# QKV stage: the remainders of queries and keys are formed by VectorE instead of GpSimd

## What is computed

```python
x = x + 0.5 * ffn(layernorm(x))
x = x + attn(layernorm(x))
x = x + 0.5 * ffn(layernorm(x))
```

```python
qkv = clip(einsum('bsd,ed->bse', layernorm(x), Wqkv), -8, 8)
q, k, v = split(qkv, 3)
q = layer_norm(q, q_ln_w, q_ln_b)        # over all 512 features
k = layer_norm(k, k_ln_w, k_ln_b)
scores = q @ k.T * 16 ** -0.5 + bias     # per head, 32 heads of 16
```

## Time and profile before

| | |
|---|---|
| median of 3 runs | 1060.15 us (1060.13 to 1060.8) |
| the profiled execution | 1064.33 us |
| its span, from first to last instruction | 1062.6 us |
| mean granted clock of TensorE, share of full speed | 0.924 |
| busy over the span: TensorE | 876.8 us, 83% |
| VectorE | 652.9 us, 61% |
| ScalarE | 446.5 us, 42% |
| GpSimd | 352.6 us, 33% |
| QKV stage, TensorE's first to last projection matmul | 274 to 459 us |

### The profile page before, as it was taken

The page is one execution under the profiler, slowest core; times in us unless marked ns, Lnnn a source line. Parts: engine busy times, 40 slices in busy tenths (PEclk is TensorE's granted clock), DMA queues, the critical chain, the costliest instruction groups (busy, mean ns, idle before and its releaser), DMA issues. The chain is left out here.

```text
span 1062.6 us, 20207 instructions
## 1 busy us (share of the span) xinstructions
PE 876.8 (83%) x6688; PEld 646.4 (61%) x6689; DVE 652.9 (61%) x1296; ACT 446.5 (42%) x818; POOL 352.6 (33%) x342
## 2 busy tenths in 40 slices
PE   2667699994698888858999999999859974699994
PEld 2556588873576776635555555555447763588873
DVE  6647244431988887757777777777427667344432
ACT  2332233331244343335777777777723430133321
POOL 4550577764022122120000000000024440577764
PEclk9997799997799999967999999999978995799998
DMA  8784578773244479664666666655148872378773
GB/s 247 268 276 119 165 142 153 140 134 50 82 152 150 154 194 207 179 203 103 145 134 140 132 138 133 140 132 112 33 140 264 292 246 99 85 142 154 135 136 52
DMA packets 112859, 162.08 MB, mean 153 GB/s; under 512 B 16864, under 2 KB 74336, under 8 KB 112512
## 3 DMA queue, kind: packets, MB, share of 16 engines
q1 hardware_dynamic: 94928, 123.85, 42.4%
q0 software_dynamic: 17856, 37.25, 19.1%
HBM read 97.44 MB, written 67.37 MB: 155 GB/s over the span
## 5 line engine op out<-in xcount | busy, mean ns | idle before, releaser
L827 DVE TENSOR_REDUCE att_part<-att_s_ps 128x2 f32<-128x1024 f32 (+2 forms) x160 | 195.4, 1225 | 61.4 <-PE att_s_ps L675 60.9
L789 ACT ACTIVATE att_prob<-att_st_ps 128x512 f32<-128x512 f32 x320 | 173.7, 595 | 78.7 <-PE att_st_ps L701 78.7
L143 PE MATMUL exp_z_ps<-ex_w_hi,exp_xT_hi 128*128 x312 | 131.7, 422 | 2.3 <-issue 1.0
L145 PE MATMUL exp_z_ps<-ex_w_hi,exp_xT_lo 128*128 x312 | 125.7, 403 | 0.0
L144 PE MATMUL exp_z_ps<-ex_w_lo,exp_xT_hi 128*128 x312 | 125.3, 402 | 0.0
L1470 DVE TENSOR_TENSOR exp_xT_lo<-exp_t_ps,exp_xT_hi 128x512 fp32r<-128x512 f32 x78 | 53.9, 692 | 106.7 <-ACT exp_xT_hi L1456 106.7
L1463 ACT ACTIVATE exp_y<-exp_y 128x512 f32<-128x512 f32 x72 | 45.5, 632 | 171.8 <-DVE exp_y L1482 171.8
L1099 POOL TENSOR_TENSOR ex_w_lo<-ex_bias,ex_w_hi 128x1024 fp32r<-128x1024 f32 x32 | 77.0, 2409 | 92.6 <-ACT ex_w_hi L1203 92.4
L1398 POOL DMA_INDIRECT exp_xg<-xn,ex_token_of x78 | 78.2, 1002 | 88.1 <-SPq L1370 60.4
L714 PE MATMUL att_pv_ps<-att_prob,att_v_sb 128*32 128x256 f32 (+2 forms) x1280 | 101.4, 391 | 1.8 <-ACT att_oT L794 1.8
L639 POOL CAST att_m_parts<-att_part 128x28 fp32r<-128x28 f32 x32 | 6.6, 208 | 271.3 <-DVE att_part L831 271.3
(11 more groups left out here) (199 smaller groups left out, 1713.4 us busy)
## 6 DMA issues: line engine op xcount, KB each, us to landing
ex_bias<-in_L_ffn_W_e SPq DMA_DIRECT2D x32, 512.0 KB, 6.8
v_vals<-st_vals SPq DMA_DIRECT2D x16, 512.0 KB, 2.8
q_parts<-st_partq SPq DMA_DIRECT2D x32, 256.0 KB, 3.4
k_parts<-st_partk SPq DMA_DIRECT2D x32, 256.0 KB, 3.8
att_v_sb<-v_vals SPq DMA_DIRECT2D x32, 256.0 KB, 3.7
ex_bias<-in_L_attn_hidden_states SPq DMA_DIRECT2D x8, 512.0 KB, 5.0
acc<-ex_bias SPq DMA_DIRECT2D x8, 512.0 KB, 7.3
xn<-route_xn SPq DMA_DIRECT2D x8, 512.0 KB, 5.9
```

The costliest lines, as they stand in the source:

```text
L143: nc.tensor.matmul(out, x_hi[:, s], w_hi(c), start=(c == 0), stop=False)
L145: last = nc.tensor.matmul(out, x_lo[:, s], w_hi(c), start=False, stop=(c == C - 1))
L789: nc.scalar.activation(prob[n % 2][:, col:col + 512], st_ps[(e + half) % 3][:, :], ACT.Exp).then_inc(exp_done, 1)
L827: nc.vector.tensor_reduce(out, src, X_AXIS, ALU.max, negate=True).then_inc(red_done, 1)
```

## The change

GpSimd's loop over the tiles is removed; GpSimd keeps its constants at the start of the stage. VectorE has a new function `rest` that forms one remainder, with the same waits and the same semaphore. In step t it runs `rest(t - 1, ..., 0)` between the normalised keys and the clip of values, and `rest(t - 1, ..., 1)` behind the clip of values; the two of the last tile stand behind the loop. VectorE's first four tiles are written out instead of two.

```diff
-            def step(t, par):
-                for s in range(2):
-                    pool.wait_ge(part_hi, 2 * t + s + 1)
-                    at_least(pool, qk_stored[par], STORES * (t // 2))
-                    nc.gpsimd.tensor_tensor(parts[s][1][par][:, :, :], whole[s][par][:, :, :], parts[s][0][par][:, :, :].bitcast(F32),
-                                            ALU.subtract).then_inc(part_lo, 1)
-            tile_loop(pool, step)
...
+            def rest(t, par, s):
+                dve.wait_ge(part_hi, 2 * t + s + 1)
+                at_least(dve, qk_stored[par], STORES * (t // 2))
+                nc.vector.tensor_tensor(parts[s][1][par][:, :, :], whole[s][par][:, :, :], parts[s][0][par][:, :, :].bitcast(F32),
+                                        ALU.subtract).then_inc(part_lo, 1)
...
             def step(t, par):
                 unit(t, par)
+                if after(t, 1):
+                    rest(t - 1, 1 - par, 0)
                 clip(t, par, 2)
-            tile_loop(dve, step)
+                if after(t, 1):
+                    rest(t - 1, 1 - par, 1)
+            tile_loop(dve, step, first=4)
+            for s in range(2):
+                rest(TILES - 1, 1, s)
```

## The result

The changed kernel takes 1047.27 us (median of 4 runs, 1046.89 to 1049.02) against 1060.47 (1060.13 to 1063.36, 4 runs) for the kernel before on the same chip: 13.2 us less. The recorded ratio is 0.9866, 95% interval 0.9842 to 0.9891; the quotient of the two medians, 0.9876, lies inside it. The profiled execution went from 1064.33 to 1049.02 us, its span from 1062.6 to 1047.3.

A forecast was written before the change was run, and what follows sets the result against it. VectorE, held partly by GpSimd, bounds the QKV stage. Gains of 6.8 us until tile 8's clip of values, 2.5 in steps 9 to 13, then 0.6 and 1.3 sum to 11.2: 1060.15 - 11.2 = 1049.0 us; range 1046.0 to 1054.6.

The forecast's parts named there:

- more is gained: Rival: VectorE's idling shrinks and TensorE keeps 2.4 GHz in the tail, giving 1046.5 to 1047.5 us; 17%.
- Blocking: GpSimd's subtractions hold VectorE's small instructions (L80, L85) until they end; removing them saves 2.0 us per ordinary step.
- The remainder's price: Each 128x512 subtraction moved to VectorE costs 0.60 us start to start, 1.2 us per step.
- The ordinary step: QKV loop step: 11.45 - 2.0 + 1.2 = 10.65 us, VectorE still bounding since TensorE needs 9.94.
- Steps 1 to 4: Early QKV steps: gains of 0.85 us in step 1, 2.4 in steps 2 and 3, 0.35 in step 4.
- Steps 9 to 13: QKV steps where VectorE waits for late loads of x: 2.5 us gained, of 3.1 if the landing keeps its distance.
- the recurrence: Steps 9 to 13: c(t) = max(c(t-1) + 1.2, c(t-2) + 14.6) + 9.45, c(t) being the start of tile t's clip of values.
- The second rival: DMA takes back the gain of steps 9 to 13: gain 8.7 us or less, 1051.5 to 1053.5 us; 22%.
- The tail: QKV stage's end after step 13: gains 0.6 us from earlier xn(15) and 1.3 with TensorE as slow as before.
- Behind c(15): From the last clip of values to attention: SP's last stores set the 8.5 us, so no gain, no loss.
- The waits of rest: VectorE's new waits for ScalarE's part and earlier stores cost nothing; ScalarE has 2 us to spare.

The follow-up runs named there:

- e1: The changed kernel with GpSimd also subtracting two idle tiles (128x512) wherever it formed a remainder before; 1065.61 us, ratio 1.0022 to the kernel before.
- e3: The changed kernel with a second 128x512 subtraction of idle SBUF tiles on VectorE behind each remainder; 1061.58 us, ratio 0.9985 to the kernel before.
- e7: The changed kernel with VectorE's first two tiles written out instead of four; 1053.09 us, ratio 0.9896 to the kernel before.
- e4: The changed kernel with SP, in steps 8 to 15, issuing query/key stores and x ahead of the stack loads, the store of values last; 1041.71 us, ratio 0.9793.
- e8: The kernel before with only SP's order changed: query/key stores and x ahead of the stack loads, store of values last; 1060.28 us, ratio 0.9948.
- e5: The kernel before, remainders still on GpSimd but each tile's waiting until the next tile's clip of values is done; 1042.0 us, ratio 0.9812.

## Why the prediction was right

The forecast was 1049.0 us, 11.2 less; the median is 1047.27, 13.2 less than that of the kernel before beside it. That lies within the stated range, but outside the 1048 to 1051 that I gave to the forecast itself: it is in the 1046.5 to 1047.5 of the case "more is gained", which had 17%. By the profiles the stage gained 3.4 us more than forecast from c(0) to c(15), in four parts of the same sign (1.2, 0.46, 0.4 and 1.4), so nothing cancelled; that the medians come within 2.0 us of the forecast is in part luck of the runs. By its steps:

**Blocking: right.** L80 and L85 are undisturbed in all steps, and e1 shows that GpSimd alone brings the blocking back.

**The remainder's price: right.** 0.60 us forecast, 0.60 in the steps of e3 and in the starts above. The 0.69 us of the Trainium skill's formula (VectorE: DVE Perf Modes, The TRN2 errata) is the length of the row, 682 to 686 ns on average, and not what the next instruction has to wait.

**The ordinary step: 10.65 forecast, 10.53 measured.** The term mis-sized is the 9.45 us that I took as VectorE's own work: in it were waits of the loop over TensorE and ScalarE that I had called unfelt. In step 9 of the kernel before, the clip of keys starts at 383.30, 0.70 behind the clip of queries at 382.60; after, the two are 0.59 apart. In the even steps 0.23 us of idling stood before the split of xT, and they are gone too. 0.11 a step, 0.46 in steps 5 to 8.

**Steps 1 to 4: 1.2 us more than forecast.** Two errors. In step 1, I counted two remainders before c(1), but that of keys lies behind it and belongs to step 2: 0.6. And in step 4 I charged 0.4 us for entering the loop, which the kernel before showed in step 2; the changed kernel shows 10.54 in step 4 and e7 10.54 in step 2. It was not VectorE's cost of entering, since neither pays it. In step 2 of the kernel before, VectorE idles 0.53 us ahead of the split of xT, against 0.23 in later even steps; why is open.

**Steps 9 to 13: right.** 58.75 us by the recurrence, 58.92 measured, in steps of 13.21, 11.00, 12.91 and 11.27 where it gave 13.4, 10.65, 13.4 and 10.65. The landing kept its distance: 14.4 and 14.6 us after c(t-2) where VectorE waited long. In steps 11 and 13 TensorE was busy throughout (11.00 and 11.27 us, at a mean granted clock of 0.90), which the recurrence left out. The second rival, DMA taking this gain back, did not come. I had taken 2.5 of the possible 3.1, and 2.9 came.

**The tail: 1.4 us more than forecast.** This is the case I held as "more is gained": the clock. After the gap of 2.67 us before 418.84 TensorE ran slow for the end of step 12 and the start of step 13, and so had no gap before the transposes at 430.18 (0.60 us for them), and the granted clock is 1.00 in steps 14 and 15. The clip of keys of 14 doesn't wait, where it waited 1.80; that of 15 waits 0.95. From there to c(15) it is 6.18 us, where I had 6.2. Tables of stretches, columns as under e4: step 14 before; steps 13 and 14 after; step 14 of e8.

```profile
442.40:454.13 11.73, 11.73 (x52) 9.54 (x51) 9.08 (x23) 4.87 (x11) 2.80 (x2) 0.90 0.43 135
```

```profile
420.21:431.48 11.27, 11.27 (x51) 9.07 (x51) 9.47 (x27) 5.15 (x12) 0.00 (x0) 0.90 0.49 156
431.48:440.06 8.58, 8.58 (x42) 6.99 (x42) 8.06 (x25) 4.28 (x10) 0.00 (x0) 1.00 0.58 183
```

```profile
441.16:451.54 10.38, 10.38 (x50) 8.45 (x49) 9.01 (x23) 4.82 (x11) 2.82 (x2) 1.00 0.48 152
```

e8 separates the two parts of this gain. It has the blocking still, but TensorE's gap before xn(15)'s transposes is 1.50 us instead of 2.69, they take 0.66 us, and the granted clock of step 14 is 1.00. Its tail from c(13) to c(15) is 19.53 us: 1.3 us less than before go with the smaller gap and the higher clock, and the 1.9 from there to the changed kernel's 17.59 are the 0.6 + 1.3 that I had forecast.

**Behind c(15): right,** 8.55 us in both; the stores set the end, and the waits of 0.7 and 1.4 us for ScalarE's last parts are under them.

**The waits of rest: right,** none before c(15).

**What was not seen** is that the profiled blocking was a matter of timing and could be had for less: e5 keeps the remainders on GpSimd and is faster than the change by its steps, 9.71 against 10.53; the intervals of the two ratios still overlap, from 0.9842 to 0.985.

## What to carry to other kernels

Where a tiny instruction of VectorE takes 1 us, look at what GpSimd is doing in the same microsecond, and see whether the two end together. Before moving GpSimd's work to a VectorE that bounds the step, try to move it in time, under VectorE's instructions with a PSUM source, or its statistics: the move paid 0.60 us for each to save 1.0, the wait paid nothing. And read a loop's waits for what they hide: twelve loads issued ahead of a wait instead of behind it were worth some 5 us.

## What the runs showed of the hardware

- A GpSimd subtraction (SBUF, 128x512, 1.3 us) holds VectorE's `tensor_scalar`, `tensor_tensor` and `scalar_tensor_tensor` within SBUF until it ends (1.26 us for one of 0.16), and doesn't hold statistics, their aggregation, clips from PSUM, or a `tensor_tensor` with one input in PSUM (0.68 and 0.69 us beside it, as alone).
- A GpSimd fill and a `tensor_scalar` within SBUF slowed each other where they met (0.83 instead of 0.54 us for the `tensor_scalar`, 0.72 instead of 0.53 for the fill); the fill did not hold two-input instructions (0.16 us).
- TensorE's step without idling is 9.71 us, shorter than the 9.94 that its busy time in a step with a gap gave. A projection matmul's row is 0.40 us long, but the next starts 0.23 after it; the last one ahead of a gap counts in full, 0.17 more. The rest comes from the transposes, which take 0.60 us when they follow at once and 0.66 behind a gap.
